# Recommendation-model MLP with pair interactions: the opening's sixteen slices divided anew between two ways of making Gram matrices, biases and W4 loaded later, three units of the second chunk moved

## The reference

```
interaction = einsum('bnd,bmd->bnm', x, x)      # 27 x 27 Gram matrix of each sample
flat = interaction[:, lower triangle without diagonal]        # 351 numbers
h = concat([x[:, 0, :], flat, 0])               # 480 features
h = relu(h @ W0.T + b0)                         # 1024
h = relu(h @ W1.T + b1)                         # 1024
h = relu(h @ W2.T + b2)                         # 512
h = relu(h @ W3.T + b3)                         # 256
out = h @ W4.T + b4                             # 1
```

## Time and profile before

| | us |
|---|---|
| median of 3 runs | 464.34 |
| lowest, highest | 463.36, 465.49 |
| the profiled execution | 465.09 |
| its span | 463.3 |
| mean granted clock in it | 0.985 |

### The profile page before, as it was taken

How to read it: one execution, slowest core, us unless ns; L and a number is a source line. 1 busy time by engine, 2 the same in 40 slices (tenths; PEclk the granted TensorE clock), 3 DMA queues, 4 the chain that set the end, 5 groups by cost and what they waited for, 6 DMA issues and landing times.

```text
span 463.3 us, 12820 instructions
## 1 busy us (share of the span) xinstructions
PE 442.6 (96%) x5815; PEld 371.5 (80%) x5815; DVE 218.2 (47%) x411; ACT 133.7 (29%) x222; POOL 0.7 (0%) x6
## 2 busy tenths in 40 slices
PE   6949979999999999999999999999999999999996
PEld 5939968878888788888888878888888879899983
DVE  3548646353437353324134334423134878656344
ACT  2635523223124222111113222111212655332241
POOL 0000000000000000000000000000000000000000
PEclk9869999999999999999999999999999999999999
DMA  8994946726326922823492024832235220460100
GB/s 308 362 403 150 367 177 214 285 67 224 132 102 221 358 55 59 312 92 134 153 403 99 1 78 170 293 136 92 95 141 177 91 91 1 136 228 2 45 1 0
DMA packets 24247, 74.77 MB, mean 161 GB/s; under 512 B 3073, under 2 KB 9217, under 8 KB 20609
## 3 DMA queue, kind: packets, MB, share of 16 engines
q1 hardware_dynamic: 24192, 73.95, 44.3%
HBM read 65.55 MB, written 8.40 MB: 160 GB/s over the span
## 4 chain that ended last, share of the span: by engine, by line
PE 89%; DVE 5%; issue 4%; ACT 1%; DMA 0%; SPq 0%; DVEq 0%; ACTq 0%
PE work L1054 18%; PE work L1056 16%; PE work L1055 16%; PE acc L1054 8%; PE acc L1056 8%; PE acc L1055 8%; PE gps L1063 7%; PE work L1081 1%; PE gps L1056 1%; PE gps L1055 1%; PE gps L1054 1%; PE acc L1081 1%; PE gps L1104 1%; DVE turned L758 1%; DVE h1l L796 1%
## 5 line engine op out<-in xcount | busy, mean ns | idle before, releaser
L1054 PE MATMUL work<-h1h,w1s 128*128 128x512 f32 (+1 forms) x208 | 81.8, 393 | 0.0
L1056 PE MATMUL work<-h1l,w1s 128*128 128x512 f32 (+1 forms) x208 | 79.5, 382 | 0.0
L1055 PE MATMUL work<-h1h,w1s 128*128 128x512 f32 (+1 forms) x208 | 79.3, 381 | 0.0
L556 ACT ACTIVATE act_out<-work,bias 128x512 f32<-128x512 f32 (+1 forms) x56 | 36.8, 657 | 111.6 <-PE work L1056 111.6
L1054 PE MATMUL work<-featH,w0l 126*128 126x512 f32 (+5 forms) x160 | 57.7, 361 | 0.5 <-issue 0.5
L1056 PE MATMUL work<-featL,w0h 126*128 126x512 f32 (+5 forms) x160 | 56.0, 350 | 1.3 <-issue 1.3
L1055 PE MATMUL work<-featH,w0h 126*128 126x512 f32 (+5 forms) x160 | 56.4, 353 | 0.0
L1054 PE MATMUL acc<-h2h,w2l 128*128 128x512 f32 x128 | 50.5, 395 | 1.0 <-DVE w2l L921 1.0
L1055 PE MATMUL acc<-h2h,w2h 128*128 128x512 f32 x128 | 49.9, 390 | 0.0
L1056 PE MATMUL acc<-h2l,w2h 128*128 128x512 f32 x128 | 49.9, 389 | 0.0
L758 DVE STREAM_TRANSPOSE turned<-grams 128x864 f32<-128x864 f32 x16 | 31.1, 1945 | 32.6 <-ACT grams L514 32.6
(11 more groups left out here) (128 smaller groups left out, 579.4 us busy)
## 6 DMA issues: line engine op xcount, KB each, us to landing
xraw<-x_t SPq DMA_DIRECT2D x48, 432.0 KB, 6.2
w1s<-w_parts SPq DMA_DIRECT2D x20, 1024.0 KB, 4.8
stage<-w_t SPq DMA_DIRECT2D x16, 512.0 KB, 5.8
w_parts<-w1s SPq DMA_DIRECT2D x8, 1024.0 KB, 4.8
xfirst<-x_t SPq DMA_DIRECT2D x9, 432.0 KB, 6.0
xmid<-x_t SPq DMA_DIRECT2D x5, 432.0 KB, 11.3
w0raw<-w_t SPq DMA_DIRECT2D x4, 512.0 KB, 10.8
w2raw<-w_t SPq DMA_DIRECT2D x4, 512.0 KB, 5.9
```

Source lines behind the costliest of these rows:

```text
L556: act.activation(act_out[:, slot(layer, m, more), cols], bank[:, cols], ACT.Relu, bias=bias[:, row:row + 1]).then_inc(relu_done, 1)
L1054: pe.matmul(dst, wl, ah, start=start, stop=False)
L1055: pe.matmul(dst, wh, ah, start=False, stop=False)
L1056: return pe.matmul(dst, wh, al, start=False, stop=stop)
```

## The change

Slices 1, 2, 4, 5, 6, 8, 9, 10 and 12 are padded, 0, 3, 7, 11, 13, 14 and 15 tiled. `xpad` has eight slots for nine padded slices; slice 12 takes slice 1's slot, and DVE waits for slice 1's Gram matrices first. `xlate` moves to a place of its own, so `xraw` lies over `xpad` alone, and `first_in_slot` now gives slice 12 for every slot. The banks are dealt anew; two banks are cleared by DVE instead of four. The orders of PE, ACT and DVE in the opening are written anew. The biases are loaded behind slice 13, W4 and b4 (one number instead of 128) behind W3, and W4 is rounded behind W3. W0's pieces are loaded after slices 8, 9, 11, 12. Chunk two's units 1 to 7 stand 3 to 7 steps later.

```diff
-FIRST_PADDED = [3, 4, 6, 7, 8]
+FIRST_PADDED = [1, 2, 4, 5, 6, 8, 9, 10, 12]
+PAD_SLOTS = 8
-            end, pads = (p + 1) * SCOLS, len(FIRST_PADDED) * SLICE_GROUPS * GROUP * QUAD
-            if end <= pads:
-                return FIRST_PADDED[(end - 1) // (SLICE_GROUPS * GROUP * QUAD)]
-            return min(FIRST_LATE + (end - 1 - pads) // SCOLS, SLICES - 1)
+            last = ((p + 1) * SCOLS - 1) // (SLICE_GROUPS * GROUP * QUAD)
+            return max(r for k, r in enumerate(FIRST_PADDED) if k % PAD_SLOTS <= last)
-        UNIT_AT = [{8: 1, 20: 2, 32: 3, 45: 4, 58: 5, 71: 6, 84: 7}] + \
+        UNIT_AT = [{14: 1, 27: 2, 39: 3, 51: 4, 63: 5, 75: 6, 87: 7}] + \
-        TURN_AT = [{26: 0, 49: 1, 75: 2, 98: 3}] + [{31: 0, 57: 1, 83: 2, 106: 3}] * (CHUNKS - 2) + [{}]
+        TURN_AT = [{34: 0, 55: 1, 79: 2, 99: 3}] + [{31: 0, 57: 1, 83: 2, 106: 3}] * (CHUNKS - 2) + [{}]
-        SMALL_AFTER = 7
-        W0_AFTER = [8, 10, 12, 13]
+        BIAS_AFTER = 13
+        W0_AFTER = [8, 9, 11, 12]
-        FIRST_BANKS = [("g0",), ("g1",), ("a0",), ("w0", "w1"), ("a0", "a1"), ("g0",), ("w0", "w1"), ("a0", "a1"),
-                       ("w0", "w1"), ("g0",), ("g1",), ("a3",), ("a0",), ("a1",), ("g0",), ("g1",)]
+        FIRST_BANKS = [("g0",), ("w0", "w1"), ("a0", "a1"), ("g1",), ("w0", "w1"), ("a0", "a1"), ("w0", "w1"), ("g0",),
+                       ("a0", "a1"), ("w0", "w1"), ("a0", "a1"), ("g1",), ("a0", "a1"), ("g0",), ("g1",), ("a3",)]
...
# SP
-                if p == SMALL_AFTER:
+                if p == BIAS_AFTER:
-                    sp.dma_start(bias[:, :], biases).then_inc(small_in, 16)
-                    sp.dma_start(w4raw[:, :, :], w4).then_inc(small_in, 16)
-                    sp.dma_start(bias4[:, :], b4.to_broadcast([P, 1])).then_inc(small_in, 16)
+                    sp.dma_start(bias[:, :], biases).then_inc(bias_in, 16)
...
             sp.dma_start(w3raw[:, :], w3).then_inc(w3_in, 16)
+            sp.dma_start(w4raw[:, :, :], w4).then_inc(w4_in, 16)
+            sp.dma_start(bias4[:, :], b4).then_inc(w4_in, 16)
...
# ACT
             for p in range(8):
                 first_from_psum(p)
-            pairs_hi_part(0, 0, True)
             w0_hi_part(0)
             first_from_psum(8)
-            first_from_psum(9)
+            pairs_hi_part(0, 0, True)
+            for p in range(9, 12):
+                first_from_psum(p)
             pairs_hi_part(0, 1, True)
-            first_from_psum(10)
-            first_from_psum(11)
             w0_hi_part(1)
             first_from_psum(12)
+            act.wait_ge(bias_in, 16)
             relu_left(0)
...
# DVE
-            for p in FIRST_PADDED[:4]:
+            for p in (4, 5, 6):
                 pad_input(p)
             pair_picks(0, 0)
             pad_input(8)
             dense_parts(0)
+            pad_input(9)
+            pair_picks(0, 1)
+            pad_input(10)
             pairs_lo_part(0, 0, True)
-            pair_picks(0, 1)
             w0_lo_part(0)
+            pad_input(12)
             pairs_lo_part(0, 1, True)
             w0_lo_part(1)
+            pair_picks(0, 2)
             split_left(0)
...
# PE
-            for p in range(8):
+            for p in range(9):
                 first_gram(p)
             transpose_pairs(0, 0, 0, True)
-            for p in range(8, 12):
+            for p in range(9, 12):
                 first_gram(p)
             transpose_pairs(0, 1, 0, True)
             first_gram(12)
             layer0_left(0)
+            layer0_left(1)
             first_gram(13)
-            layer0_left(1)
             layer0_left(2)
+            layer0_left(3)
             first_gram(14)
-            layer0_left(3)
+            layer0_left(4)
+            transpose_pairs(0, 2, 0, True)
             first_gram(15)
-            transpose_pairs(0, 2, 0, True)
-            layer0_left(4)
             layer0_left(5)
```

More of the change, by code:

```diff
@@ L105, in rec_program @@
         bias = sb("bias", [P, MT0 + MT1 + MT2 + MT3])
-        bias4 = sb("bias4", [P, 1])
+        bias4 = sb("bias4", [1, 1])
         ident = sb("ident", [P, P])
@@ L125, in rec_program @@
         w3h = sb("w3h", [P, KT3 * SIZES[3]], f32r)
+        with nc.sbuf_tensor("xlate", [P, SLICES - FIRST_LATE, SCOLS], f32) as xlate:
+            pass
         w1s = sb("w1s", [P, 2, 2, KT1 * P], f32r)
@@ L146, in rec_program @@
             pass
-        with nc.sbuf_tensor("xpad", [P, len(FIRST_PADDED), SLICE_GROUPS * GROUP, QUAD], f32) as xpad, \
-                nc.sbuf_tensor("xlate", [P, SLICES - FIRST_LATE, SCOLS], f32) as xlate:
+        with nc.sbuf_tensor("xpad", [P, PAD_SLOTS, SLICE_GROUPS * GROUP, QUAD], f32) as xpad:
             pass
@@ L163, in rec_program @@
         gps = ctx.enter_context(nc.psum_tensor("gps", [P, 2, BANK], f32))
-        small_in = sem("small_in")
+        bias_in, w4_in = sem("bias_in"), sem("w4_in")
         w0_in = [sem(f"w0_in{n}") for n in range(W0_LOADS)]
@@ L540, in pairs_hi_part @@
                 act.wait_ge(pairs_t, SUBS * g + s + 1)
+                if first and s == 0:
+                    act.wait_ge(zero_done, 2)
                 dst = featH[0:PAIRS_TILE, 1:KT0, s * SUB:(s + 1) * SUB]
@@ L621, in _ @@
             act.wait_ge(table_in, 1)
-            act.wait_ge(zero_done, 2)
             for p in range(8):
                 first_from_psum(p)
-            pairs_hi_part(0, 0, True)
             w0_hi_part(0)
             first_from_psum(8)
-            first_from_psum(9)
+            pairs_hi_part(0, 0, True)
+            for p in range(9, 12):
+                first_from_psum(p)
             pairs_hi_part(0, 1, True)
-            first_from_psum(10)
-            first_from_psum(11)
             w0_hi_part(1)
             first_from_psum(12)
+            act.wait_ge(bias_in, 16)
             relu_left(0)
-            first_from_psum(13)
             w0_hi_part(2)
             relu_left(1)
+            first_from_psum(13)
             relu_left(2)
-            first_from_psum(14)
             w0_hi_part(3)
             relu_left(3)
+            first_from_psum(14)
+            relu_left(4)
+            pairs_hi_part(0, 2, True)
             first_from_psum(15)
[L643 to L646, removed]
             relu_left(5)
-            w1_hi_part(0)
             relu_left(6)
@@ L651, in _ @@
             relu_left(7)
+            w1_hi_part(0)
             grams_from_psum(1, 0)
@@ L676, in on_step @@
                         w3_hi_part()
+                        act.wait_ge(w4_in, 32)
+                        act.activation(w4s[:, :, 0:1], w4raw[:, :, :], ACT.Copy).then_inc(w4_hi, 1)
                 def last_layers():
@@ L720, in _ @@
             dve.memset(gps[:, :, 0:UNIT_GROUPS * INPUTS], 0.0).then_inc(banks_zero, 1)
-            for name in ("a0", "a3"):
-                dve.memset(BANKS[name][:, 0:FIRST_COLS], 0.0).then_inc(banks_zero, 1)
+            dve.memset(BANKS["a3"][:, 0:FIRST_COLS], 0.0).then_inc(banks_zero, 1)
             dve.memset(xpad[:, :, :, INPUTS:], 0.0).then_inc(xpads_zero, 1)
@@ L774, in pad_input @@
                     dve.wait_ge(xpads_zero, 1)
-                dve.tensor_copy(xpad[:, k, :, 0:INPUTS], first_slot(p).rearrange("p (b n) -> p b n", n=INPUTS))\
-                   .then_inc(xpad_done, 1)
+                if k >= PAD_SLOTS:
+                    dve.wait_ge(gram_done, FIRST_PADDED[k - PAD_SLOTS] + 1)
+                dve.tensor_copy(xpad[:, k % PAD_SLOTS, :, 0:INPUTS],
+                                first_slot(p).rearrange("p (b n) -> p b n", n=INPUTS)).then_inc(xpad_done, 1)
             def pairs_lo_part(g, s, first=False):
@@ L926, in w3_lo_part @@
                 dve.tensor_tensor(w3l[:, :], w3raw[:, :], w3h[:, :].bitcast(f32), ALU.subtract).then_inc(w3_done, 1)
+            pad_input(1)
+            pad_input(2)
             dve.memset(featH[:, KT0 - 1, :].bitcast(f32), 0.0).then_inc(zero_done, 1)
@@ L955, in _ @@
             split_left(7)
-            dve.wait_ge(w4_hi, 1)
-            dve.tensor_tensor(w4s[:, :, 1:2], w4raw[:, :, :], w4s[:, :, 0:1].bitcast(f32), ALU.subtract)\
-               .then_inc(w4_done, 1)
+            w1_lo_part(0)
             def body(c, more):
@@ L993, in on_step @@
                         w3_lo_part()
+                        dve.wait_ge(w4_hi, 1)
+                        dve.tensor_tensor(w4s[:, :, 1:2], w4raw[:, :, :], w4s[:, :, 0:1].bitcast(f32), ALU.subtract)\
+                           .then_inc(w4_done, 1)
                 def last_layers():
@@ L1071, in first_gram @@
                     pe.wait_ge(x_first[p], 16)
-                    pe.wait_ge(banks_zero, 3)
+                    pe.wait_ge(banks_zero, 2)
                     ge(pe, grams_out, banks_used(p))
@@ L1078, in first_gram @@
                 for k in range(SLICE_GROUPS):
-                    four = xpad[:, FIRST_PADDED.index(p), k * GROUP:(k + 1) * GROUP, :]
+                    four = xpad[:, FIRST_PADDED.index(p) % PAD_SLOTS, k * GROUP:(k + 1) * GROUP, :]
```

8 lines of the change are left out of this document (3 added, 5 removed).

## The result

| | before | after |
|---|---|---|
| median, us | 464.42 | 458.7 |
| lowest to highest | 463.36 to 465.49 | 456.55 to 459.89 |
| the profiled execution | 465.09 | 456.55 |
| its span | 463.3 | 454.7 |
| mean granted clock in it | 0.985 | 0.998 |

The ratio is 0.987, with a 95% interval of 0.983 to 0.992: 1.3% faster. Run again on another occasion the changed kernel had a median of 457.49 against 464.43, ratio 0.984 (0.982 to 0.987). The forecast was 456.2 for the median and 457.0 for the profiled execution; the profiled one took 456.55 and was the fastest of the eight executions of the changed kernel, while the one of before (465.09) lay above its median.

The account below looks back on a forecast made before the run. PE bounds the kernel, 96% busy, with idle from code fetches and work at low clock. From 465.09 us, 17.7 removed and 9.6 added, net -8.1, gave 457.0, less 0.75 for the median 456.2; range 452.0 to 461.5.

Parts of the forecast that it names:

- Rival 4: Stalls are not fetches and stay, 11.35 us; only 5.0 of work added and 1.0 saved, 468.3 us; chance 0.05.
- The 1.61, 3.22, 3.50, 1.28 and 1.74: PE's five "issue" stalls in us before 68 us, 11.35 together, read as code fetches; 3.3 of fetch stalls to stay.
- border 1218: PE's instruction 1218, start of layer 0's left half's tile 4: needed at 34.2, there at 35.3, 1.1 us stall left.
- border 1730: PE's instruction 1730, 16 behind chunk two's first unit: needed at 45.2, there at 47.4, 2.2 us stall left.
- Waits for slice 1, slice 10, slice 12 and the last transposes: PE's waits in the opening for copies, ACT's emptied banks and last picks: 0.4, 0.1, 0.4, 0.4, together 1.3 us.
- Wait for w2l: PE's 1.0 us wait for W2's second part goes, since it is rounded before unit 5's picks, now at step 63.
- the 1.6 us for the low clock before 15.5 us: Regained at full clock in the opening: a padded slice takes 1.95 us instead of 3.56.
- I take full clock throughout: PE nearly without a break keeps full clock; 1.6 us back before 15.5 and 2.3 in 26 to 36, sum 3.9.
- rival 1: Fetches stay a bound elsewhere, or DVE does, 1 to 2 us each, clock drop 1.6 more; 460.7 us; chance 0.16.
- the 0.75 us taken off for the median: Median of runs was 0.75 below the profiled execution, so the forecast went from 457.0 to 456.2.
- The small transfers: Moving them off slice 7 saves some 2.4 us of transfer; slices 8 to 15 land about 2 earlier, not counted.
- Rival 3: PE held at 1.2 GHz during padded slices, 1.6 us more each, nine are 14.5, 470.7 in all; chance 0.06.

Follow-up runs that it names:

- moved borders: Changed kernel with a warm-up of 9 transposes and 16 small matmuls instead of 15 transposes, 52 PE instructions more; 463.74 us, ratio 0.997.
- tiled slices side by side: Changed kernel with slices 9 and 10 tiled again, so 9, 10 and 11 stand together, 192 instructions more; 458.02 us, ratio 0.986.
- units-only: Kernel before with the new steps of chunk two's units and turns alone; 464.42 us, ratio 0.999.
- small-transfers kernel: Kernel before with only biases moved behind slice 13, W4 and b4 behind W3, W4's rounding behind W3's; 464.60 us, ratio 1.001.
- new opening: Changed kernel with the old steps of units and turns; 464.69 us, ratio 1.000.
- second profile: The changed kernel unaltered, profiled once more on another occasion; median 457.49 us, ratio 0.984.
- another kernel with the same program up to there: Changed kernel with old unit steps except units 3 and 4 at 39 and 51, second turn at 55; 460.77 us, ratio 0.989.
- kernel with the unit moved: Changed kernel with chunk two's first unit behind layer 0's right halves 0 and 1, on PE and ACT; 455.84 us (0.980), again 455.96 (0.982).

## Why the prediction was right, and where it wasn't

**The bound and the count: right.** The stalls are code fetches of 256 instructions; moved borders moved them (111 matmuls against 110), and tiled slices side by side brought them back at the counted places. Rival 4 fell. The Trainium skill says that the cost of a border is mostly hidden ("Runtime: NRT & Kernel Launch", Instruction fetch mechanics). That agrees with the number of borders, of which 41 of 43 in the changed kernel and 40 of 45 in the kernel before passed without a stall of 0.5 us, and not with the cost of the others, up to 5.34 us at one border.

**The walk through the opening: close in each term of the profiled execution, the total partly by luck.** The 1.61, 3.22, 3.50, 1.28 and 1.74 went. At border 1218: 1.1 expected, 1.35 there. At border 1730: 2.2 expected, 1.93 there. Waits for slice 1, slice 10, slice 12 and the last transposes: 0.4, 0.1, 0.4, 0.4 expected, 0.26, 0.30, 0.44, 0.33 there. Left half from 27 us: 26.51. Wait for w2l: gone. Net 8.1 expected, 8.5 there (465.09 to 456.55). But this compares a slow execution of before with the fastest one of after; the medians differ by 5.7 and 6.9. Two terms were not fixed: the 1.6 us for the low clock before 15.5 us were not lost in the profiles of the units-only and the small-transfers kernel (clock 1.00 from 11 to 16 us, with the old opening), and the wait for slice 10, expected at 0.1, was 0.30 to 0.95. The prediction's "twelve products" are twelve matmuls, four products as the kernel's section has it; their times are right.

**The median: 2.5 us above the forecast in the first set, 1.3 in the second.** The range holds both. Two steps of the prediction are off. The first is "I take full clock throughout": the low clock behind a remaining stall stood only in rival 1. Behind stalls of about 2 us the clock falls in some executions and not in others. It stayed behind 1.93 here, 2.04 (new opening) and 2.06 (units only), and fell behind 1.93 and 1.95 (new opening), 2.21 (second profile) and 2.37 (units only). The second profile prices it at 1.5 to 1.7 us. The second step is the 0.75 us taken off for the median, because before's profiled execution had been slow by as much; here the profiled one was the fast one.

The clock is not the whole of it. The other executions of the first set had spans of 458.1, 457.0 and 456.8 at clocks of 0.994 to 0.996, against 454.7 at 0.998. A mean of 0.995 over 457 us is 4.6 us at half clock, up to 2.3 us of lost work, and 0.998 is 0.9, so the clock can explain some 1.4 of the 2.3 us between them. But in the second set an execution at 1.000 took 457.56 us and one at 0.994 took 457.43. What else varied there wasn't profiled; the two profiles show 0.65 in the wait for slice 10's copy, and the stall at tile 4 reached 2.88 in another kernel with the same program up to there. The kernel with the unit moved has a shorter second stall and no low clock behind it in either profile, and its medians, 455.84 and 455.96, lie close to its profiled executions (456.00 and 455.74).

**The shares of the parts: wrong in reading.** The sum of the prediction books about 4 us for the opening and 4 for the units and w2l. Alone each is worth nothing measurable. The units' new steps are right for the borders of the new opening only; with the old opening they make stalls of 2.37 and 2.06, and the new opening with the old steps makes 2.04 and 1.95. The expectation for the old steps stopped counting at border 2498 and so missed both. With units 3 and 4 alone at their new steps (the title of this document speaks of three units; the change moves seven) most of the gain was there: ratio 0.989 against 1.000.

**The small transfers: right to count at nothing**; 1.001 alone. Their size was read too high: the two windows of the earlier trace rows at 158 and 191 GB/s instead of 400 are 1.1 us of lost transfer, not 2.4, and slice 15 landed at 28.6 in the changed kernel instead of 29.8, 1.2 us sooner and not 2. **DVE:** it kept pace but for the wait for slice 10 above. **Rival 3** (held at half clock under padded slices): the padded slices took 1.93 to 2.04 us in the changed kernel, and the clock was 1.00 from 26 to 33 us in both profiles.

## What to carry to other kernels

When "issue" idle stands in the middle of a run of small matmuls, count instructions and look for a packet of the instruction queue before PE resumes. Here all such stalls stood on multiples of 256 instructions and were code fetches, and the cure was either fewer instructions for the work or slower work between two borders, by placing dense bursts (a tiled unit is 256 instructions in 1.27 us) where long products stand around them. Such a change has to be judged as a whole and to the end of the region, since each instruction added or removed moves every later border; test the parts together, and look for the stall that appears tens of us later. The count tells where a stall can stand, not that it will. In the changed kernel the borders 4802 and 5058 lay 1.3 us apart (160.0 and 161.3) and PE did not stall, because the packet for the second had started at 157.6, before the first was passed; what decides how early a fetch starts is open. A remaining idle stretch of 1 to 2 us costs more than its length, because the clock may fall behind it.

## What the runs showed of the hardware

- Every one of the 40 "issue" stretches of PE of 0.5 us or more in the fourteen traces stands at instruction 450 plus a multiple of 256 (or one behind), with a packet of 16 KB of the instruction queue starting 2.2 to 2.6 us before PE resumes. The changed kernel has 43 such borders and 44 packets.
- The stall at a border was up to 5.34 us, with 1.3 us of work between two borders and the DMA engines full (24 to 28 us, 398 GB/s). Its length at one place varied between executions: 1.05, 1.35, 1.93 and 2.88 us at the left half's tile 4, with the same PE program up to there.
- Behind a stall of 1.93 us the clock stayed at 2.4 GHz in one execution; behind 2.21 us at the same place it fell to 1.2 GHz in another. Behind 2.37 us it fell and behind 2.06 us it stayed, in one trace.
- A float32 matmul of 8 columns with a 128x128 weight took 0.21 us in the warm-up (32 in 6.84 us), nearly as long as a transpose of 128 columns there (9 in 2.18 us, 0.24 each). The first padded slice behind them took 3.75 us, the second 2.06, while the windows give a granted clock of 1.00 for both; so at the very start of a trace that column doesn't tell how fast PE ran.
